# A decoder layer with routed experts: a tile's rows are turned between gate and up of the tile ahead

## The reference, cut to what matters

```
h = _rms(x, w_ln2).reshape(B * S, H)
logits = h @ w_router
probs = jax.nn.softmax(logits, axis=-1)
top_w, top_i = jax.lax.top_k(probs, TOP_K)                    # 2 of 8 experts
combine = jnp.sum(jax.nn.one_hot(top_i, N_EXP) * top_w[..., None], axis=1)
g = jnp.einsum('th,ehi->eti', h, w_gate_e)                    # 512 -> 352
u = jnp.einsum('th,ehi->eti', h, w_up_e)
y = jnp.einsum('eti,eih->eth', jax.nn.silu(g) * u, w_down_e)  # 352 -> 512
routed = jnp.einsum('eth,te->th', y, combine)
sh = jax.nn.silu(h @ w_sh_gate) * (h @ w_sh_up) @ w_sh_down   # 512 -> 1408 -> 512
sh = sh * jax.nn.sigmoid(h @ w_sh_eg)
x = x + (routed + sh).reshape(B, S, H)
```

## Time and profile before

| | us |
|---|---|
| median of 3 runs | 2609.94 (2604.54 to 2612.02) |
| the profiled execution | 2617.23 |
| its span | 2615.5 |
| TensorE busy in it | 2417.4 (92%) |
| VectorE, ScalarE, POOL busy | 1358.2 (52%), 1347.7 (52%), 909.6 (35%) |

### The profile page before, as it was taken

The page is one execution under the profiler, slowest core; times in us unless marked ns, Lnnn a source line. Parts: engine busy times, 40 slices in busy tenths (PEclk is TensorE's granted clock), DMA queues, the critical chain, the costliest instruction groups (busy, mean ns, idle before and its releaser), DMA issues. The chain is left out here.

```text
span 2615.5 us, 39055 instructions
## 1 busy us (share of the span) xinstructions
PE 2417.4 (92%) x15376; PEld 1555.7 (59%) x15376; DVE 1358.2 (52%) x2114; ACT 1347.7 (52%) x1708; POOL 909.6 (35%) x592
## 2 busy tenths in 40 slices
PE   7996989999999999999997999998799999999897
PEld 5885644444444444444334565555588888888786
DVE  5566534434344434333414556555655666666775
ACT  4231457667766777767993444333322355554221
POOL 1224744656456545554112333331140112121220
PEclk8998899999999999999998999999899999999999
DMA  5002674576638654754736000010262366665330
GB/s 177 17 1 78 190 214 119 135 200 171 152 92 223 162 149 108 208 157 130 175 83 209 1 1 17 1 49 23 73 215 73 128 217 224 229 212 176 120 122 35
DMA packets 208006, 331.45 MB, mean 127 GB/s; under 512 B 71312, under 2 KB 125840, under 8 KB 207632
## 3 DMA queue, kind: packets, MB, share of 16 engines
q1 hardware_dynamic: 190608, 256.99, 34.7%
q0 software_dynamic: 15056, 68.03, 7.8%
q10 hardware_dynamic: 2160, 3.93, 0.5%
HBM read 241.53 MB, written 99.42 MB: 130 GB/s over the span
## 5 line engine op out<-in xcount | busy, mean ns | idle before, releaser
L938 ACT ACTIVATE A_c_prob<-c_psum 128x1024 f32<-128x1024 f32 x832 | 787.1, 1029 | 291.1 <-PE c_psum L1188 286.4
L864 POOL TENSOR_TENSOR c_rr<-c_ms,c_half 128x32 f32<-128x32 f32 (+1 forms) x72 | 372.5, 5177 | 434.4 <-DVE c_ms L955 434.4
L1197 PE MATMUL c_psum<-A_c_prob,c_vq 128*17 128x512 f32 x3328 | 416.5, 600 | 11.1 <-DVE c_oT L1092 9.4
L134 PE MATMUL c_psum<-R_c_w,S_c_c 128*128 128x512 f32 x1248 | 314.9, 402 | 1.5 <-DVE S_c_t L1018 1.0
L1188 PE MATMUL c_psum<-c_qq,c_kq 64*128 64x512 f32 x1664 | 289.9, 440 | 19.6 <-ACT A_c_prob L938 11.3
L134 PEld LDWEIGHTS c_psum<-R_c_w,S_c_c 128*128 128x128 f32 x1248 | 228.7, 189 | 124.7 <-issue 43.2
L1188 PEld LDWEIGHTS c_psum<-c_qq,c_kq 64*128 64x128 f32 x1664 | 137.6, 186 | 169.4 <-ACT A_c_prob L938 90.5
L134 PE MATMUL m_psum<-R_m_t,m_up_hi 128*128 128x256 f32 (+1 forms) x1104 | 205.0, 286 | 23.9 <-DVE R_m_t L2313 23.9
L2358 PE MATMUL m_psum<-A_m_dn_hi,A_m_a 128*128 128x512 f32 (+1 forms) x628 | 205.1, 396 | 12.8 <-DVE A_m_a L2167 12.8
L995 DVE COPY Q_c_unit<-c_psum 128x256 f32<-128x256 f32 x89 | 37.8, 425 | 333.7 <-PE c_psum L134 333.7
L1616 DVE TENSOR_REDUCE s_topx<-s_psum 128x4 f32<-128x2048 f32 (+1 forms) x64 | 95.5, 1492 | 176.7 <-PE s_psum L1719 173.3
(11 more groups left out here) (296 smaller groups left out, 4344.1 us busy)
## 6 DMA issues: line engine op xcount, KB each, us to landing
c_kq<-kd SPq DMA_DIRECT2D x248, 208.0 KB, 5.9
kd<-S_c_t SPq DMA_DIRECT2D x96, 256.0 KB, 3.5
Q_c_raw<-in_ctxT SPq DMA_DIRECT2D x89, 256.0 KB, 4.9
qd<-A_c_q SPq DMA_DIRECT2D x64, 256.0 KB
c_qq<-qd SPq DMA_DIRECT2D x64, 256.0 KB, 3.1
vd<-A_c_vt SPq DMA_DIRECT2D x104, 136.0 KB, 2.9
c_vq<-vd SPq DMA_DIRECT2D x31, 442.0 KB, 8.9
R_m_hs<-slots SPq DMA_DIRECT2D x23, 512.0 KB, 7.4
```

The source lines that it names most:

```text
L134: mm = pe.matmul(out, a(c), b(c), start=first and i == 0, stop=last and i == len(terms) - 1)
L864: pool.tensor_tensor(rr[:, unit % RB, 0:n], ms[:, unit % RB, 0:n], half[:, 0:n], ALU.pow).then_inc(s_r, 1)
L938: act.activation(prob[:, t % PB, 2 * (u % 2):2 * (u % 2) + 2, :], score_banks[u % 3], ACT.Exp, scale=XD ** -0.5).then_inc(s_ex, 1)
L1197: mm = pe.matmul(o_bank[32 * j:32 * j + VW, :], vq[:, q % 2, kt, j, :], prob[:, t % PB, j, :], start=kt == 0, stop=kt == CT - 1)
```

## The change

In a pass that is followed by a routed tile, TensorE turns that tile between gate and up of chunk 1, where it did so behind up. ScalarE makes the turned rows' high parts ahead of chunk 1's rounding, and in a routed pass it splits the down weights behind them, where it did so ahead of chunk 1's sigmoid. VectorE makes the low parts ahead of gating chunk 1, and in a routed pass splits the down weights between gating chunk 1 and its low part. A shared pass keeps its split of the down weights where it was.

```
@@ ScalarE @@
-                if first[w] == p and w:
+                if first[w] == p and w and x.shared:
                     split_down(w)
                 if not single:
                     sigmoid(1)
-                    high_act(1)
                 if p + 1 < NP and not passes[p + 1].shared:
                     high_rows(passes[p + 1].tile)
+                if not x.shared:
+                    split_down(w)
+                if not single:
+                    high_act(1)
                 if len(x.chunks) > 2:
                     sigmoid(2)
                     high_act(2)
@@ VectorE @@
+            def low_rows(tile):
+                for k in range(KC):
+                    dve.wait_ge(s_thi, KC * tile + k // 2 * 2 + 2)
+                    dve.scalar_tensor_tensor(t_lo[tile % 2][:, k, :], t_bank[k // 2][:, (k % 2) * TW:(k % 2 + 1) * TW], w2[:, k:k + 1],
+                                             t_hi[tile % 2][:, k, :], ALU.mult, ALU.subtract).then_inc(s_tlo, 1)
...
-                if first[w] == p and w:
+                if first[w] == p and w and x.shared:
+                    split_down(w)
+                if p + 1 < NP and not passes[p + 1].shared:
+                    low_rows(passes[p + 1].tile)
+                if not single:
+                    gated(x, 1)
+                if not x.shared:
                     split_down(w)
                 if not single:
-                    gated(x, 1)
                     low_act(x, 1)
...
-                if p + 1 < NP and not passes[p + 1].shared:
-                    tile = passes[p + 1].tile
-                    for k in range(KC):
...
@@ TensorE @@
                         if n == 0:
                             pe.wait_ge(s_uplo[j], 1)
+                        if i == 1 and j == 1 and p + 1 < NP and not passes[p + 1].shared:
+                            turn(passes[p + 1].tile)
                         product3(pe, gu_bank[n % 2][j][0:rows, 0:width],
...
-                        if p + 1 < NP and not passes[p + 1].shared:
-                            turn(passes[p + 1].tile)
```

More of the change, by code:

```diff
@@ L2308, in _ @@
                     combine(p, late + 1)
-                if p + 1 < NP and not passes[p + 1].shared:
-                    tile = passes[p + 1].tile
-                    for k in range(KC):
-                        dve.wait_ge(s_thi, KC * tile + k // 2 * 2 + 2)
-                        dve.scalar_tensor_tensor(t_lo[tile % 2][:, k, :], t_bank[k // 2][:, (k % 2) * TW:(k % 2 + 1) * TW], w2[:, k:k + 1],
-                                                 t_hi[tile % 2][:, k, :], ALU.mult, ALU.subtract).then_inc(s_tlo, 1)
                 if len(x.chunks) > 2:
```

## The result

| | us |
|---|---|
| median before, 4 runs beside the changed kernel | 2610.98 (2604.54 to 2612.04) |
| median after, 4 runs | 2578.23 (2575.08 to 2579.25) |
| ratio | 0.9873, 95% interval 0.9858 to 0.9887 |
| profiled execution after, its span | 2578.19, 2576.5 |

The changed kernel is faster by 1.3%. The forecast was 2580.5 in a range of 2574 to 2595. In the profile after, down is L2366 (before L2358), the turn L2344 (L2336), the low parts of the turned rows L2266 (L2313), the low part of the activation L2170 (L2167).

The account below looks back on a forecast made before the run. TensorE was taken as the bound, with one hole a pass; 5.6 us at the first tile plus 21 x (14.782 - 13.65) = 23.8 gave 29.4 us saved, a median of 2580.5 us, range 2574 to 2595.

Parts of the forecast that it names:

- The bound: Regular routed passes: TensorE is the bound, busy 290.13 of 310.43 us, with one hole in each pass of 14.782 us.
- TensorE's own sum: TensorE's matmuls and turn in a routed pass: 2.86 + 4.14 + 2.85 + 0.80 + 2.91 = 13.56 us without a wait.
- The queues of ScalarE and VectorE: Start and end times of both engines' reordered steps in a pass, from high parts at 9.20 to chunk 2's low part at 16.36.
- The tie ahead of down: Next pass's down: chunk 2's low part reaches TensorE after 9.31 us, its weight load comes at 9.30; pass taken as 13.65.
- The first tile: Start of the routed passes: no idle time or clock dip, so tile 1 starts at 2072.60 instead of 2078.21, 5.6 us saved.
- The DMAs: Down gather issued later, at 14.2 + 0.27 instead of 11.35, with 3.2 us to spare; costs nothing.
- C: Rival: a down gather landing in over 10 us decides over TensorE; at 12.5 us, 2632 us in all; chance 0.03.
- The sum: Whole kernel: 5.6 us at the first tile plus 23.8 over 21 passes, 29.4 us saved.
- bound A: Rival: the wait moves to the down product, 0.5 us plus 0.1 restart, a pass of 14.15, 2591 us; chance 0.17.

Follow-up runs that it names:

- e4: The changed kernel with the split of the down weights left where it was before, on ScalarE and VectorE; 2582.49 us, ratio 0.9889 to the kernel before.
- e5: The changed kernel with one more VectorE subtraction behind chunk 1's low part in each routed pass; 2589.36 us, ratio 0.9912 to the kernel before.
- e6: The kernel before with the change only in the last shared pass, for tile 0; 2608.13 us against 2611.85, ratio 0.9987.
- e3: The kernel before with only TensorE's turn moved, ScalarE and VectorE in their old orders; 2611.75 us against 2609.72, ratio 1.0004.
- e8: The changed kernel with the down weights' gather issued behind the up gathers of the tile after next; 2725.3 us, ratio 1.0435 to the kernel before.
- e2: The changed kernel with the turn left behind up of chunk 1, only the new ScalarE and VectorE orders kept; 2614.95 us against 2609.72, ratio 1.0021.

## Why the prediction was right

**The bound.** Right. TensorE had one hole a pass, and without it a pass is the sum of its matmuls.

**TensorE's own sum.** 13.56 forecast without a wait; 13.53 in e4, where nothing waits.

**The queues of ScalarE and VectorE.** High parts forecast at 9.20 us of a pass, measured 9.22; low parts 10.05 and 10.10; down weights' low half ready 14.19 and 14.21; chunk 2's low part ready at 16.36 and 16.41. Sums over ten operations held because each was read from the same instruction in the trace of before, with the overlap or gap to its neighbour.

**The tie ahead of down.** Shown. Forecast was a pass of 13.65, between 13.56 (just in time) and 13.75 (a load exposed); measured 13.635, the first matmul of down spaced by 0.07 more, and e5 shows that what is added to the chain is added to the pass. The Trainium skill's rule on weight loads that are pulled ahead of running matmuls (TensorE: Matmul & The Clock Gate, "Step-by-step: what each phase is for") points the right way: the load's lead shrank from 0.12 to 0.03 us. Its price was less than the whole load of 0.19 that I had put for it: 13.635 against 13.53, 0.1. That 13.65 met 13.635 so closely is in part luck: it was picked between two bounds 0.2 us apart, and a chain a tenth longer would have come out as a wait.

**The first tile.** 5.6 forecast, 5.6 measured. That the lower clock came from the idle time is shown by e6, where it goes with it, and by e3, where the wait is 3.9 us and the clock is 1.2 GHz again from 2060 to 2063. TensorE's turn of tile 1 didn't wait for X: the additions end at 2058.48, the turn's first matmul is at 2058.56 in the timeline. That was met with 0.08 us to spare.

**The DMAs.** Right, with room: the down gather is wanted at about 24.3 us and is there at 14.5 + 4.9 = 19.4. e8 shows that a late gather is dear. It was late there by being issued late; the case that C feared, a gather in its present place that takes over 10 us, was seen in no run.

**The sum.** 29.4 forecast, 29.7 in the trace's own stretches, 28.7 to 29.2 in the experts' of three traces. The median came out 2.3 us lower than forecast, the profiled execution 9.6 lower (2587.8 forecast, 2578.19). The step that was off there is "I take the same saving off both": the profiled execution of before was long because its experts began at 1868.1, at the late end of the scatter, and that did not repeat.

**What was wrong.** One sentence, in what it leaves out: "The halves are late because they are queued behind chunk 1's activation, not because the turn is late." Of the halves it is true: e2 takes the queueing away and leaves the turn, and the wait for them is gone from the regular passes. But e2 is 5 us slower than before. Once the halves stand first in the queue, they hold back everything behind them until the turn is there, and the chain through chunk 1's gating to down becomes the bound. Both had to move. The sum did not suffer, since it was made for both moves together. The price of a new wait was too low as well: bound A took 0.1 us for the restart, and by the rows of e2 and before a stop costs some 0.27 beyond its idle time. And the third move, the split of the down weights, which I costed without asking whether it was needed, was not (e4).

## What to carry to other kernels

When a product waits for an operand that is queued behind other work, work out where each engine's queue stands in both orders, start by start, and look for who is late next: here that gave the size of the gain and the tie that limits it. Moving work to the head of an in-order queue pays only if its input is there by then; otherwise all that stood ahead of it is late as well. Where the stages ahead of a change scatter by more than the effect in doubt, compare a stretch of the trace that starts at the change's own stage.

## What the runs showed of the hardware

The clock's part was larger than expected where idle times come back: waits of 3.1 to 5.6 us in each pass of e8 brought the granted clock to 0.90 on the mean, while 0.97 a pass before, and one of 2.25 in e2, left it at 1.00. A single wait lowers it too, and the lower clock comes when the work has already resumed. Before, TensorE waits 3.06 us and resumes at 2061.03; it has the full clock at first, then 1.2 GHz for over 3 us, then 2.4 again:

```profile
2061.03:2061.50 0.47, 0.47 (x4) 0.47 (x5) 0.00 (x0) 0.00 (x0) 0.00 (x0) 1.00 0.13 48
2062.00:2065.00 3.00, 3.00 (x17) 3.00 (x16) 0.43 (x1) 1.65 (x2) 0.00 (x0) 0.50 0.00 0
2065.50:2066.50 1.00, 1.00 (x7) 0.83 (x6) 0.73 (x2) 0.28 (x1) 0.00 (x0) 1.00 0.00 0
```

A gather of 786 KB took 4.9 us to land when issued by itself (the up gathers and the row load landed within some 1 us of its issue), 6.6 behind two others that had 4 us of lead, and 8.9 right behind them. So the prediction's estimate of 3.8 us for a gather that is alone was 1.1 us short.
